# The down product of a mixture-of-experts kernel in three matmuls of 256 columns for every tile

## The reference, cut to what matters

```python
h = jax.nn.gelu(jnp.einsum('bsd,edh->bseh', x, w1) + b1, approximate=False)
expert_out = jnp.einsum('bseh,ehd->bsed', h, w2) + b2
sel = jnp.take_along_axis(expert_out, top_i[..., None], axis=2)
return (top_p[..., None] * sel).sum(axis=2)
```

## Time and profile before

| what | value |
|---|---|
| median of 3 runs | 298.06 us (297.62 to 298.1) |
| profiled execution | 296.99 us, of which the span 295.2 us |
| busy: TensorE, its weight loads | 91%, 75% of the span |
| busy: VectorE, ScalarE, GpSimd | 65%, 66%, 59% |
| granted TensorE clock, mean | 0.965 of full speed |
| tiles 8 to 38 | from about 114 us to 281 us |

### The profile page before, as it was taken

How to read it: one execution, slowest core, us unless ns; L and a number is a source line. 1 busy time by engine, 2 the same in 40 slices (tenths; PEclk the granted TensorE clock), 3 DMA queues, 4 the chain that set the end, 5 groups by cost and what they waited for, 6 DMA issues and landing times.

```text
span 295.2 us, 8972 instructions
## 1 busy us (share of the span) xinstructions
PE 269.6 (91%) x3065; PEld 221.2 (75%) x3065; DVE 191.9 (65%) x430; ACT 195.2 (66%) x425; POOL 175.4 (59%) x160
## 2 busy tenths in 40 slices
PE   7899967899999999999999999999999989999800
PEld 5778957788799998877778777777777767877500
DVE  2957787799999897656655655555656555556510
ACT  3355469499897997677667676766776756776500
POOL 8200026833366989887777877767787657464340
PEclk9799996999999999999999999999999999999985
DMA  6799995499862234645535555534535434332220
GB/s 160 290 400 388 368 323 155 129 404 450 294 191 41 38 59 69 95 76 88 93 56 91 75 93 73 79 68 76 90 59 80 88 56 74 53 39 25 32 35 1
DMA packets 39881, 39.53 MB, mean 134 GB/s; under 512 B 19920, under 2 KB 35744, under 8 KB 39680
## 3 DMA queue, kind: packets, MB, share of 16 engines
q1 hardware_dynamic: 32320, 28.56, 31.7%
q0 software_dynamic: 7488, 10.39, 21.9%
q10 hardware_dynamic: 32, 0.01, 0.0%
HBM read 27.61 MB, written 9.64 MB: 126 GB/s over the span
## 4 chain that ended last, share of the span: by engine, by line
PE 73%; DVE 9%; issue 6%; DMA 5%; POOL 4%; ACT 0%; DVEq 0%; POOLq 0%
PE ps L639 30%; PE ps L656 28%; DVE wsp L940 5%; PE ps L537 5%; DMA out<-onehot,idx 4%; PE ps L555 3%; POOL out L468 2%; PE ps L648 1%; POOL onehot L459 1%; PE ps L479 1%; PE ps L615 1%; DMA rows<-y_rows,idx 1%; PE ps L510 1%; PE ps L519 1%; DVE dv L871 1%
## 5 line engine op out<-in xcount | busy, mean ns | idle before, releaser
L639 PEld LDWEIGHTS ps<-onehot,wsp 128*128 (+1 forms) x1872 | 130.0, 98 | 37.4 <-issue 2.9
L639 PE MATMUL ps<-onehot,wsp 128*128 128x128 f16 x1872 | 154.4, 219 | 1.8 <-issue 1.5
L818 ACT ACTIVATE pay<-ps,cur 128x128 f32<-128x128 f32 x312 | 117.5, 463 | 54.9 <-issue 39.9
L656 PE MATMUL ps<-wsp,pay 128*128 (+1 forms) x616 | 139.4, 316 | 1.2 <-DVE pay L1102 1.2
L468 POOL DMA_INDIRECT out<-onehot,idx x39 | 68.7, 1762 | 28.9 <-POOL onehot L459 12.1
L1102 DVE SCALAR_TENSOR_TENSOR pay<-pay,cur 128x512 f16<-128x512 f32 x72 | 54.9, 762 | 28.8 <-ACT pay L806 26.6
L437 POOL DMA_INDIRECT rows<-y_rows,idx x39 | 49.4, 1266 | 22.4 <-issue 11.0
L459 POOL TENSOR_SCALAR onehot<-onehot,cur 128x256 f32<-128x256 f32 x37 | 43.0, 1161 | 25.6 <-DVE onehot L1120 21.6
L656 PEld LDWEIGHTS ps<-wsp,pay 128*128 128x128 f16 x616 | 45.3, 97 | 5.0 <-issue 1.6
L1096 DVE TENSOR_SCALAR pay<-pay,cur 128x512 f16<-128x512 f32 x36 | 19.4, 538 | 26.4 <-ACT pay L818 24.1
L806 ACT ACTIVATE pay<-pay,cur 128x512 f16<-128x512 f32 x36 | 26.0, 722 | 1.2
(11 more groups left out here) (177 smaller groups left out, 193.0 us busy)
## 6 DMA issues: line engine op xcount, KB each, us to landing
stage<-in_L_ffn_w SPq DMA_DIRECT2D x9, 1024.0 KB, 9.9
wsp<-in_L_ffn_w SPq DMA_DIRECT2D x7, 1024.0 KB, 11.8
y_rows<-pay SPq DMA_DIRECT2D x4, 512.0 KB, 9.4
wsp<-in_x SPq DMA_DIRECT2D x3, 512.0 KB, 8.1
b2bc<-in_L_ffn_b SPq DMA_DIRECT2D x1, 1024.0 KB, 9.4
rows<-y_rows,idx POOLq DMA_INDIRECT x39
out<-onehot,idx POOLq DMA_INDIRECT x39
wsp<-in_x SPq DMA_DIRECT2D x2, 256.0 KB, 5.8
```

Of the source, the lines that this page charges most:

```text
L639: last = mm(ps[:, HB + (2 * j + g) % RING, c * P:(c + 1) * P], wsp[:, bass.ds(e, 1), o:o + P].rearrange("p a f -> p (a f)"), xsp[:, j % RI ...
L656: last = mm(ps[:, OB + j % 2, 0:width], hsp[:, (2 * j + g) % NH, part, c, :], wsp[:, bass.ds(e, 1), o + w:o + w + width].rearrange("p a f ...
L818: last = a.activation(to, ps[:, HB + (2 * j + g) % RING, c * P:(c + 1) * P], ACT.Gelu, bias=cur[:, j % CURS, cc:cc + 1], scale=cur[:, j % ...
```

## The change

`EARLY` is gone. Every tile from 3 on has the three matmuls of 256 columns, and its rows are made by one VectorE operation; the semaphore `o_sum` and the second operation are gone.

```diff
-EARLY = 8
...
-                if j < EARLY:
-                    steps = ((0, 0, D), (0, D, D), (1, 0, D))
-                else:
-                    steps = ((0, 0, 2 * D), (1, 0, D))
+                steps = ((0, 0, D), (0, D, D), (1, 0, D))
                 for q, (part, w, width) in enumerate(steps):
                     last = mm(ps[:, OB + j % 2, 0:width], hsp[:, (2 * j + g) % NH, part, c, :],
                               wsp[:, bass.ds(e, 1), o + w:o + w + width].rearrange("p a f -> p (a f)"),
...
                 v.scalar_tensor_tensor(out=outb[:, r, :], in0=ps[:, OB + j % 2, 0:D], scalar=cur[:, j % CURS, C_O:C_O + 1],
                                        in1=b2bc[:, bass.ds(e, 1), :].rearrange("p a d -> p (a d)"),
-                                       op0=ALU.mult, op1=ALU.add).then_inc(o_read if j < EARLY else o_sum, 1)
-                if j >= EARLY:
-                    dve.wait_ge(o_sum, j - EARLY + 1)
-                    v.scalar_tensor_tensor(out=outb[:, r, :], in0=ps[:, OB + j % 2, D:2 * D], scalar=cur[:, j % CURS, C_O:C_O + 1],
-                                           in1=outb[:, r, :], op0=ALU.mult, op1=ALU.add).then_inc(o_read, 1)
+                                       op0=ALU.mult, op1=ALU.add).then_inc(o_read, 1)
```

More of the change, by code:

```diff
@@ L248, in adaln_moe @@
         l1_done = sem("l1_done"); gelu_done = sem("gelu_done"); h_high0 = sem("h_high0"); h_high1 = sem("h_high1")
-        h_split = sem("h_split"); l2_done = sem("l2_done"); o_sum = sem("o_sum"); o_read = sem("o_read"); o_ready = sem("o_ready"); o_last = sem("o_last")
+        h_split = sem("h_split"); l2_done = sem("l2_done"); o_read = sem("o_read"); o_ready = sem("o_ready"); o_last = sem("o_last")
         added = sem("added")
```

## The result

The changed kernel takes 328.42 us (median of 4 runs, 326.2 to 328.61); the kernel before, measured beside it, 297.84 us (297.35 to 298.1). The ratio is 1.101, with a 95% interval of 1.096 to 1.106: slower by 30.6 us. The profiled execution has a span of 326.9 us against 295.2.

The account below looks back on a forecast made before the run. TensorE's sequencer, computing weight addresses, was taken to bound the tile loop. +30.9 us for one more address per step, +0.04 for the last twelve steps and -0.5 in the tail made +30.4, forecast 328.4 us, range 325.3 to 332.

Parts of the forecast that it names:

- The bound: Tile loop from tile 8: TensorE's sequencer, computing five addresses per step, sets the 0.673 us pitch; the array needs 0.660.
- The price of an address: Down matmuls, tiles 8 to 38: one more address adds 0.131 us per step over 236 steps, +30.9 us.
- The reading from one moment with an empty queue: At 193 us five address computations took 0.62 us, 0.124 each; loads and matmuls between them are issued for nothing.
- The 0.007 us: Per step of the loop: three more instructions' share of the sequencer's 0.053 us of other halts, added to 0.124.
- The address is kept: Down matmuls: the last o is not computed anew, so two computations per step there, six in all, 496 in total.
- The lead: The sequencer's head start from the constant-address stage is only used up sooner; it does not change the +30.9 us.
- The rule of the sum: The sequencer's whole work grows by 236 x 0.131 us, and it paces both kernels at the end.
- The tail: After the loop: without the second VectorE operation, tile 36's weighting and the last scatters move up, -0.5 us.
- Part 2: Removing the second VectorE operation and its wait: nothing in the loop, -0.5 us in the tail; tile 37's rows stay covered.
- The base: Starting time for the sum: profiled execution 296.99 us gives 327.4, the three runs' median 298.06 gives 328.5; stated 328.4.
- The signs: Profile after: 496 computations, 864 matmuls at the down line, tiles 6.4 us apart, lower TensorE busy share, scatters 4 to 5 apart.
- The rule against the sum: Issue floor of about 20 cycles per instruction: 24 instructions take 0.40 us per step, hiding the new address; chance 0.05.

Follow-up runs that it names:

- narrow_one_addr: Changed kernel, but the second of the three down matmuls rereads the high weights, so one address per step at the down line: 298.3 us, ratio 1.002.
- wide_two_addr: Kernel before, but the second down matmul reads weights from o+D, one address more per step and nothing else: 328.95 us, ratio 1.107.
- narrow_three_addr: Changed kernel, but the third down matmul reads from o+128, a third address per step at the down line: 359.22 us, ratio 1.208.
- wide_four_addr: Kernel before, but the sixth up matmul reads the fifth's weights, four addresses per step instead of five: 294.51 us, ratio 0.991.

## Why the prediction was right, point by point

**The bound.** The step that carried everything was that the sequencer, not the array, paces tiles 8 to 38. Shown from both sides: an address more costs 31.8 us in the medians with nothing else changed, an address fewer gains 2.7 us in the medians (5.3 in the trace of the loop) and brings the step to 0.660.

**The price of an address.** Taken 0.131 us per step with the two instructions beside it. Measured 30.75 us over the 235 steps between the two rows, 0.131. The step is 0.806 us, forecast 0.804. The reading from one moment with an empty queue (0.62 us for five) was enough: in the middle of the changed kernel's loop, too, loads that each wait for a new address are 0.12 to 0.13 us apart. It also said rightly that the matmul and load beside it are issued for nothing, which narrow_one_addr shows (0.676 against 0.673). The 0.007 us that the sum adds for three instructions' share of the halts had the right size but was shared out wrongly: wide_two_addr, with the address alone, has 0.803 us per step, 0.130 above before, so nearly all of it comes with the address. Why the halts grow with it no run tells.

**The address is kept.** 496 computations, as assumed; 744 would have given the 359 us that narrow_three_addr has.

**The lead.** Used up after four or five steps. The rule of the sum, that it counts for nothing because the sequencer paces both kernels at the end, held: the 30.75 us contain it.

**The tail** was forecast too small: -0.5, and measured -1.47. Of that, 0.93 is the start of the scatter of tile 36 against the last group (0.65 ahead instead of 0.28 behind): the operation gives 0.5, and the other 0.4 is an error of counting. Tile 36's rows are ready some three to four steps before the last step with up matmuls, so those steps are not on the chain any more, and 236 should have been 232 or 233 there. Part 2 saw that these steps move TensorE against the scatter, but only asked whether they make the rows of tile 37 late. The last 0.5 us are the scatters' own distances, 4.49 and 4.25 us where before had 4.82 and 4.46. They need not come from the change: narrow_one_addr, with the same single VectorE operation, has 5.17 and 4.40. What makes a landing shorter was not tried.

**The base.** The forecast of 328.4 us stood on the median of 298.06; on 297.84 it would have been 328.2. The agreement with 328.42 to less than 0.1 us is luck: the single runs spread over 2.4 us, and with the loop and tail as the traces have them (29.3 us) the sum would have been 327.1. The tail's error of 1 us was made good by the 1.3 us that the medians have beyond the traces' loop and tail.

**The signs.** 496 computations, 864 matmuls, tiles 6.4 us apart and the last three scatters 4 to 5 us apart came as forecast. The lower busy share of TensorE in the loop came too, but by 0.4 points (98.6% against 99.0%), too little to recognise a step that is 20% longer.

**The rule against the sum.** The run with the address alone is 31.8 us slower, so the address was not hidden. By the issue floor that the Trainium skill's "Runtime: NRT & Kernel Launch", section Instruction fetch mechanics, gives, it would have been. The measurement decides against using that floor as the price of a register computation. Nor did plain instructions add up by it: the load and the matmul that narrow_one_addr has more cost 0.003 us per step. By that floor they would be an estimated 0.03 us, from the prediction's 0.40 us for 24 instructions against 0.35 for 21. Whether they were issued within another instruction's time no run tells.

**Left open.** With four addresses the gain on before is 0.9% (0.6 to 1.2), with one instruction for all 1.85% (1.5 to 2.2), though the loop has the same 0.660 us per step in both. The traces put the difference outside the loop: the stretch of 154.98 us in wide_four_addr is 155.12 in the wide kernel with one instruction (115.14 to 270.26), while the start of that stretch and the end after it vary between executions, and the two were measured in different sets of runs. What the 0.08 us beside a register computation are was not looked at beyond their size: a price of every register instruction, or a wait of the next load for the value it has just written.

## What to carry to other kernels

Where weights are addressed through a register, count the separate addresses and not only the matmuls: here each separate computation cost the sequencer 0.112 to 0.124 us, more than the 0.055 us per 128-column matmul (six in 0.33 us). With the sequencer pacing the loop, the split of one matmul in two was dear only because the second half needed an address of its own. A stretch whose pitch is above the array's, at full clock and without a releaser, was the sign; a moment just after the queue ran empty gave the price. What helped was to compute the addresses of a step together, ahead of it.

## What the runs showed of the hardware that was not expected

Most of the price is not the arithmetic: one addition (32 ns busy) held the sequencer 0.112 us, three fused operations (46 ns) 0.124 us, and one instruction with the addresses of a whole step (74 ns) brought a step of 0.737 us down to the array's 0.6625. A sequencer with a lead also hides what had cost time between batches: the tile with the wait for eight expert numbers took 6.09 us before and 5.28 us with four addresses. And TensorE's busy share of the span rose from 91% to 92% while it did the same arithmetic 10% more slowly, because the lost time lies in a loop where it counts as 98.6% busy all the same.
